# Packing a short inner tile, keeping four output pieces for the end, and pacing row loads in a three-stage decoder layer

## The chip, the cores and the metric

The kernel is one program on one core of a Trainium2 chip. Its engines are TensorE (PE in the profile; its weight loads are PEld), VectorE (DVE), ScalarE (ACT), GpSimd (POOL) and SyncE (SP), which here issues every DMA. The metric is the device time of one execution in microseconds; lower is better.

## The reference, cut to what matters

The input x is (8, 256, 1024), that is 2048 tokens of 1024 values. Three blocks follow each other, each added to the stream after a layer norm:

```python
x = x + attn(layernorm(x))        # 32 heads, 8 key/value heads; weights are sign(w), a scale per output channel
x = x + xattn(layernorm(x), ctx)  # low-rank cross attention, 16 heads
x = x + ffn(layernorm(x))

def bitnet_linear(x, weight, scale_param):
    s = jnp.maximum(jnp.mean(jnp.abs(weight), axis=1), 1e-08)
    return jnp.einsum('bsi,oi->bso', x, jnp.sign(weight / s[:, None])) * (s * scale_param)

def ffn(x):                       # U1 (1024, 256), V1 (256, 2*2752), U2 (2752, 256), V2 (256, 1024)
    H = (x @ U1) @ V1 + b1
    act = silu(H[..., :2752]) * H[..., 2752:]
    return (act @ U2) @ V2 + b2
```

The inner width 2752 is 21 tiles of 128 and one of 64.

## The kernel before, in words

The 2048 tokens are worked in four groups (`NG`) of 512 (`GT`). The three stages follow each other; the results of the first two pass through DRAM (`x1_scratch`, `x2_scratch`). One list, `ORDER`, sets the order of all work: `self_order`, `cross_order` and `ffn_order` write it by hand, and each engine's program walks through the same list and does its own share of every step, in that order, with semaphores between the engines. So a step that waits on an engine holds back all later steps of that engine, and that holds for SyncE's DMA issues too.

**Self-attention.** A group has 64 head steps (slots); work for the next group is put beside them by slot number (`put`). After each projection of queries or keys (`q_out`, `k_out`) its high and low float32r parts are copied by three DMAs of 256 KB into a stack (`q_stack`, `k_stack`) that the score matmuls (L804, L824) read. Row tiles of 512 KB (`load`, `wload`, `o_load`) go through two rings of buffers, `xin` and `x_res`. The channel scales of the v and o weights are needed as rows that are the same in all partitions: for each 128 channels VectorE makes a diagonal matrix (L1310) and TensorE multiplies ones by it (L755), four times for one PSUM bank; VectorE copies that out (L1332). For v (`row_v`) this happens in the start-up, for o (`row_o`) at the end of group 0, between the last queries (L790) and the keys of group 1 (L765). Two PSUM banks are then in turn for all such steps.

**Feed-forward.** A float32 product is done as three float32r matmuls (`PASSES`: high by high, high by low, low by high). For each group: `down` (48 matmuls), then for each of 22 inner tiles `gu` (gate and up, one bank each, 12 matmuls, L1002), SiLU on ScalarE (L1208), product on VectorE (L1513), high copy on ScalarE (L1212), low part on VectorE (L1516), and `z` (6 matmuls, L1014), which adds into two banks. TensorE does `gu` of a tile before `z` of the tile before it. The weights of each tile are split by ScalarE and GpSimd (`iw`: L1189, L1617) and by ScalarE and VectorE (`dw`: L1198, L1505). The short tile is padded with zeros, which GpSimd writes (L1596, L1614). At a group's end come `z` of the last tile and `z_out` (two copies L1220, two low parts L1522). The eight output pieces `y` of a group (6 matmuls each, L1027) stand in the first tiles of the next group; each `y_out` is two VectorE steps, row plus bias (L1533) and matmul plus row (L1536). Those of group 3 come at the end. `y_load` brings the rows (L1656), and a whole row of 512 KB is stored when its second piece is done (L1774, L1772).

Of the kernel before, what the change touches and what calls it, by code (L numbers as in the profile page):

```python
# [14 lines left out]
P = 128  # L15
# [31 lines left out]

AHEAD = 3
# [54 lines left out]
def self_order():  # L103
# [18 lines left out]
    order += signs(VB + 1) + flip_sign(VB) + with_inside(q_parts(0, 0), 4, flip_sign(VB + 1))  # L122
# [8 lines left out]
    for g in range(NG):  # L131
# [12 lines left out]
        if g == 0:  # L144
# [71 lines left out]
        if g == 0:  # L216
            order += [("row_o", 0), ("row_o_out", 0), ("row_o", 1), ("row_o_out", 1)]
# [80 lines left out]
def ffn_order():  # L298
    order = [("u2_zero",), ("iw_load", 0), ("b1_load",), ("iw_load", 1)]
# [6 lines left out]
    for g in range(NG):  # L306
        plan = {f: [] for f in range(FB)}
        if g:
            for i in range(2 * TILES):
                plan[i + 1].append([("y", g - 1, i), ("y_out", g - 1, i)])  # L310
                if i in (1, 3):
                    plan[i + 2].append([("y_load", g - 1, i // 2 + 2)])
# [13 lines left out]
        plan[FB - 2].append([("y_load", g, 0)])  # L326
        plan[FB - 1].append([("y_load", g, 1)])
        if g == NG - 1:
            plan[FB - 1] += [[("y_load", g, 2)], [("y_load", g, 3)]]
        for f in range(FB):  # L330
# [53 lines left out]
def row_buffers():  # L384

    out, before, last, count = {}, {}, {}, {"xin": 0, "xres": 0}
    for step in ORDER:
# [5 lines left out]
        elif step[0] in ("o_load", "v2_load") or step in (("u1_load", 0), ("raw_load", 1)):  # L393
            ring = "xres"
        elif step[0] == "y_load":
            ring = "xin" if step[1] == NG - 1 and step[2] >= 2 else "xres"
        else:
            continue
# [22 lines left out]
XSTACK = ordinals("xq_out")  # L421
STORES = {}
# [23 lines left out]
def build_program(nc, x, ctx_in, wq, qs, wk, ks, wv, vs, wo, os_, wq_d, w_qk, wkv_d, wv_u,  # L446
# [6 lines left out]
    def semaphore(name):  # L453
# [93 lines left out]


    names = ("consts scale_landed scale_mixed scale_cols abs chan mean_dve sign sign_set diag row_set "
# [5 lines left out]
             "u2_zero b1_zero b1_landed b1_set b2_landed u1_hi u1_lo p_hi p_lo v2_hi v2_lo "  # L555
             "iw_zero iw_hi iw_lo dw_hi dw_lo gate_up silu inner inner_hi inner_lo z_done z_hi z_lo y_dve").split()
# [19 lines left out]
    def copied_out(kind, *at):  # L576
# [31 lines left out]
        return sem["y_dve"], 2 * (at[0] * 2 * TILES + at[1]) + 2  # L608
# [97 lines left out]

    RAW_SPLIT = {1: 2, 0: 3, 2: 4, 3: 5}
    ROW_FIRST = {"v": (VB, KT), "o": (OB, KB)}
    row_numbers = {("v", 0): 0, ("o", 0): 1, ("o", 1): 2}
    diag_first = {("v", 0): 0, ("o", 0): KT, ("o", 1): KT + 4}  # L710


    def tensor_program(e):
        pe = e.eng
        for kind, *at in ORDER:
# [30 lines left out]
            elif kind in ("row_v", "row_o"):  # L746
                which = kind[-1]
                J, full, use = bank_of(kind + "_out", *at)
                n = min(4, ROW_FIRST[which][1])
                e.wait_ge(sem["consts"], 4)  # L750
                bank_free(e, kind + "_out", *at)
                for i in range(n):
                    d = diag_first[which, at[0]] + i
                    e.wait_ge(sem["diag"], d + 1)
                    t = pe.matmul(J[:, i * P:(i + 1) * P], ones[:, :], tmp[d % 2][:, 0:P], start=True, stop=True)  # L755
                    t.then_inc(full, 1) if i == n - 1 else t.then_inc(sem["row_set"], 1)
# [234 lines left out]
            elif kind == "gu":  # L991
# [4 lines left out]
                for s in range(2):  # L996
# [7 lines left out]
                    t.then_inc(sem["gate_up"], 1)  # L1004
            elif kind == "z":
# [6 lines left out]
                for r in range(RB):  # L1012
                    for wp, ap in PASSES:
# [4 lines left out]
            elif kind == "y":  # L1018
# [6 lines left out]
                for r in range(RB):  # L1025
                    for wp, ap in PASSES:
                        t = pe.matmul(J[:, :], zT[ap][:, r, m * P:(m + 1) * P], v2s[wp][:, r, n * GT:(n + 1) * GT],  # L1027
# [4 lines left out]
    def scalar_program(e):  # L1032
        act = e.eng
        for kind, *at in ORDER:
# [145 lines left out]
            elif kind == "iw":  # L1180
                g, f = at
                W = g * FB + f
                n = P if f < FB - 1 else FLAST
# [3 lines left out]
                if n < P:  # L1187
                    e.wait_ge(sem["iw_zero"], 2 * (g + 1))
                act.activation(v1s[W % 3][0][:, :, :, 0:n], inner_gu(f, n), ACT.Copy).then_inc(sem["iw_hi"], 1)  # L1189
            elif kind == "dw":  # L1190
                g, f = at
                W = g * FB + f
                e.wait_ge(iw_landed[f // CB], iw_total(f // CB))
                if W > 2:
                    e.wait_ge(sem["z_done"], W - 2)
                if f == FB - 1:
                    e.wait_ge(sem["u2_zero"], 1)
                act.activation(u2s[W % 3][0][:, :, :], u2_all[:, f, :].rearrange("p (r n) -> p r n", r=RB),  # L1198
                               ACT.Copy).then_inc(sem["dw_hi"], 1)
            elif kind == "gu":  # L1200
                g, f = at
                W = g * FB + f
                a = inner[W % 2]
# [4 lines left out]
                act.activation(a[:, :], bank[2 * W % 4][:, :], ACT.Silu, bias=b1c[:, f:f + 1]).then_inc(sem["silu"], 1)  # L1208
# [3 lines left out]
                act.activation(inner_hl[W % 2][:, 0, :], a[:, :], ACT.Copy).then_inc(sem["inner_hi"], 1)  # L1212
            elif kind == "z_out":
                g = at[0]
                e.wait_ge(sem["z_done"], FB * (g + 1))
                if g:
                    _, full, use = bank_of("y_out", g - 1, 2 * TILES - 1)
                    e.wait_ge(full, use + 1)
                for r in range(RB):
                    act.activation(zT[0][:, r, :], z_banks[r][:, :], ACT.Copy).then_inc(sem["z_hi"], 1)  # L1220

    def iw_total(c):
        return 16 * (3 if (c + 1) * CB * P <= INTER else 4)
# [16 lines left out]
    def vector_program(e):  # L1240
        dve = e.eng
        for kind, *at in ORDER:
# [54 lines left out]
            elif kind in ("row_v", "row_o"):  # L1297
                which = kind[-1]
                first, n = ROW_FIRST[which]
                for i in range(min(4, n)):  # L1300
                    idx = first + 4 * at[0] + i
                    d = diag_first[which, at[0]] + i
                    e.wait_ge(sem["chan"], SIGN["sign", idx] + 1)
                    e.wait_ge(sem["consts"], 3)
                    if which == "o" and i < 2:
                        _, full, use = bank_of("row_o_out" if at[0] else "row_v_out", 0)
# [520 lines left out]
```

## Time and profile before

| | |
|---|---|
| runs | 1490.9 us median of 3 (1489.54 to 1490.96) |
| the profiled execution's own time | 1487.3 us |
| its span, first to last instruction | 1485.5 us |
| TensorE busy | 1361.7 us (92%) |
| VectorE, ScalarE, GpSimd busy | 908.5, 709.9, 516.5 us |
| mean granted TensorE clock | 0.993 |

The profiled execution is one execution, recorded by the hardware; busy times are unions of the instructions of an engine. A matmul's recorded duration includes the passage through the array, so in a stream they overlap: 512-column matmuls of 0.39 us start closer together than that. A number in square brackets behind a timeline row is the idle time of the engine just before it and what ended it.

### The profile page before, as it was taken

To read this page: it belongs to the slowest core of one execution; us is meant where nothing else is said; L and a number is where in the kernel's file an instruction comes from. 1 tells how busy PE (TensorE), PEld (TensorE's weight loads), DVE (VectorE), ACT (ScalarE), POOL (GpSimd) and SP (SyncE) were. 2 spreads that over 40 slices of the span, in tenths; PEclk is the share of its full clock that TensorE was granted. 3 is DMA by queue.
4 is the path that set the end of the run, shared out by engine and by line. 5 is a ranking of instruction groups with operands and counts; after the bars stand their busy time and mean duration, and the time that the engine had idled before them with its cause. 6 is when DMAs were issued, how large, how long until landed. Compare 5 with 4: busy or idle time off the path is not lost.

```text
span 1485.5 us, 22620 instructions
## 1 busy us (share of the span) xinstructions
PE 1361.7 (92%) x8423; PEld 969.2 (65%) x8423; DVE 908.5 (61%) x1615; ACT 709.9 (48%) x1589; POOL 516.5 (35%) x457
## 2 busy tenths in 40 slices
PE   6788899899989998898889798778999999999998
PEld 4555455545555555557667676667888887887886
DVE  5578556835683668667486584663754754763645
ACT  4376503540354145437567475664544354354352
POOL 2047503760476156602121121123432432342230
PEclk9999899999999999999999999999999999999999
DMA  5786645665548455365546364436300310310121
GB/s 150 143 167 130 117 78 123 94 96 107 111 76 121 108 111 114 102 194 151 153 102 171 92 169 111 129 100 232 136 10 15 116 41 1 114 57 1 71 71 57
DMA packets 94881, 157.55 MB, mean 106 GB/s; under 512 B 9910, under 2 KB 49076, under 8 KB 94772
## 3 DMA queue, kind: packets, MB, share of 16 engines
q1 hardware_dynamic: 94772, 156.11, 44.1%
q8 instruction: 67, 1.10, 0.3%
q14 instruction: 42, 0.34, 0.1%
HBM read 82.15 MB, written 25.17 MB: 72 GB/s over the span
## 4 chain that ended last, share of the span: by engine, by line
PE 65%; DVE 12%; DMA 10%; ACT 5%; issue 5%; SPq 2%; POOL 1%; DVEq 0%; POOLq 0%; ACTq 0%
PE bank L1002 16%; PE bank L1014 8%; PE bank L918 7%; DMA q_stack<-hi_lo 5%; PE bank L790 5%; PE bank L903 3%; PE bank L744 3%; PE bank L824 3%; PE bank L839 2%; PE bank L804 2%; PE bank L1027 2%; PE bank L876 2%; PE bank L987 2%; PE bank L888 2%; PE bank L765 2%
## 5 line engine op out<-in xcount | busy, mean ns | idle before, releaser
L1556 POOL TENSOR_TENSOR fold<-wide 128x512 f32<-128x512 f32 x128 | 164.1, 1291 | 240.5 <-ACT wide L1082 221.3
L1082 ACT ACTIVATE wide<-bank 128x512 f32<-128x512 f32 x256 | 151.3, 597 | 141.7 <-PE bank L824 139.5
L1617 POOL TENSOR_TENSOR v_lo<-v_all,v_hi 128x512 fp32r<-128x512 f32 x88 | 122.7, 1395 | 233.6 <-ACT v_hi L1189 233.6
L1364 DVE TENSOR_REDUCE neg_top<-bank 128x2 f32<-128x512 f32 x256 | 171.0, 681 | 52.9 <-PE bank L804 51.5
L824 PE MATMUL bank<-q_stack,k_stack 98*128 98x512 f32 x256 | 138.4, 541 | 3.4 <-ACT wide L1082 2.6
L1002 PE MATMUL bank<-pT_hi,v_hi 128*128 128x512 f32 x352 | 137.3, 390 | 1.2 <-POOL v_lo L1617 1.2
L1002 PE MATMUL bank<-pT_hi,v_lo 128*128 128x512 f32 x352 | 137.2, 390 | 0.0
L1002 PE MATMUL bank<-pT_lo,v_hi 128*128 128x512 f32 x352 | 136.9, 389 | 0.0
L1513 DVE SCALAR_TENSOR_TENSOR inner<-bank,b_cols,inner 128x512 f32<-128x512 f32 x88 | 65.9, 749 | 111.3 <-PE bank L1002 108.0
L804 PE MATMUL bank<-k_stack,q_stack 96*128 96x256 f32 x512 | 111.0, 304 | 15.4 <-DMA q_stack<-hi_lo 9.7
L1099 ACT ACTIVATE wide<-bank,neg_max 128x256 f32<-128x256 f32 x256 | 120.0, 488 | 7.3 <-DVE neg_max L1392 7.3
L804 PEld LDWEIGHTS bank<-k_stack,q_stack 96*128 96x128 f32 x512 | 93.0, 193 | 44.1 <-DMA q_stack<-hi_lo 15.1
L1212 ACT ACTIVATE inner_hl<-inner 128x512 fp32r<-128x512 f32 x88 | 55.6, 632 | 135.3 <-DVE inner L1513 135.3
L1014 PE MATMUL bank<-inner_hl,u_hi 128*128 128x512 f32 x352 | 111.4, 397 | 3.7 <-DVE inner_hl L1516 3.7
L1593 POOL TENSOR_TENSOR x_group<-x_group,tmp 128x512 f32<-128x512 f32 x32 | 41.8, 1306 | 193.8 <-DVE tmp L1473 193.8
L1392 DVE TENSOR_REDUCE neg_max<-bank 128x2 f32<-128x512 f32 x128 | 86.8, 683 | 34.5 <-PE bank L876 33.8
L790 PE MATMUL bank<-hT_hi,signs_qkv 128*128 128x512 f16 x256 | 100.1, 391 | 5.0 <-DVE signs_qkv L1266 5.0
L1516 DVE TENSOR_TENSOR inner_hl<-inner,inner_hl 128x512 fp32r<-128x512 f32 x88 | 65.0, 739 | 61.5 <-ACT inner_hl L1212 61.5
L1208 ACT ACTIVATE inner<-bank,b_cols 128x512 f32<-128x512 f32 x88 | 60.5, 687 | 82.2 <-PE bank L1002 82.0
L1564 POOL TENSOR_TENSOR bn<-bn,neg_half 128x1 f32<-128x1 f32 x48 | 30.4, 632 | 197.5 <-DVE bn L1282 197.4
L918 PE MATMUL bank<-signs_o,attnT_hi 128*128 128x512 f16 x256 | 97.5, 381 | 0.8 <-DVE tmp L1413 0.6
L790 PE MATMUL bank<-hT_lo,signs_qkv 128*128 128x512 f16 x256 | 98.0, 383 | 0.0
(178 smaller groups left out, 3114.5 us busy)
## 6 DMA issues: line engine op xcount, KB each, us to landing
q_stack<-hi_lo SPq DMA_DIRECT2D x96, 256.0 KB, 6.4
xin<-x_scratch SPq DMA_DIRECT2D x32, 512.0 KB, 4.6
xq_stack<-xhi_lo SPq DMA_DIRECT2D x128, 128.0 KB, 2.4
x_res<-in_x SPq DMA_DIRECT2D x21, 512.0 KB, 5.0
x_scratch<-x_res SPq DMA_DIRECT2D x16, 512.0 KB, 2.9
xin<-in_ctx SPq DMA_DIRECT2D x16, 512.0 KB, 4.7
x_res<-x_scratch SPq DMA_DIRECT2D x16, 512.0 KB, 4.2
x_group<-x_scratch SPq DMA_DIRECT2D x32, 256.0 KB, 3.3
```

The costliest lines, as they stand in the source:

```text
L790: t = pe.matmul(J[:, :], sW[:, kb, tq * P:(tq + 1) * P], hT[p][:, kb, :], start=kb == 0 and p == 0, stop=kb == KB - 1 and p == 1)
L804: t = pe.matmul(tops[n % 2][:, a * SEQ:(a + 1) * SEQ], qst[U % Q_STACKS][0:SUB, r, b * SEQ + a * P:b * SEQ + (a + 1) * P], kst[0:SUB, tq, ...
L824: pe.matmul(tiles[m % 2][:, :], kst[0:SUB + 2, tq, b * SEQ + kt * P:b * SEQ + (kt + 1) * P], qst[U % Q_STACKS][0:SUB + 2, 2 * hp:2 * hp + ...
L918: t = pe.matmul(J[:, :], OT[p][:, tq, m * P:(m + 1) * P], sWo[:, tq, n * GT:(n + 1) * GT], start=tq == 0 and p == 0, stop=tq == KB - 1 and ...
L1002: t = pe.matmul(G[:, :], v1s[W % 3][wp][:, s, r, :], pT[g % 2][ap][:, r, :], start=r == 0 and (wp, ap) == (0, 0), stop=r == RB - 1 and wp ...
L1014: t = pe.matmul(z_banks[r][:, :], u2s[W % 3][wp][:, r, :], inner_hl[W % 2][:, ap, :], start=f == 0 and (wp, ap) == (0, 0), stop=f == FB - ...
L1082: act.activation(PT[m % PT_RING][:, :], tiles[m % 2][:, :], ACT.Exp).then_inc(sem["tile_exped"], 1)
L1099: t = act.activation(Pb[:, a * SEQ:(a + 1) * SEQ], S[:, a * SEQ:(a + 1) * SEQ], ACT.Exp, bias=mx[:, a:a + 1], accum_out=total)
L1364: dve.tensor_reduce(neg_top[U % 2][:, r, b, :], tops[n % 2][:, :].rearrange("p (a b) -> p a b", a=QT), AX.X, ALU.max, negate=True).then_in ...
L1392: dve.tensor_reduce(neg_max[n % 4][:, 0:QT], scores[n % 3][:, :].rearrange("p (a b) -> p a b", a=QT), AX.X, ALU.max, negate=True).then_inc ...
L1556: pool.tensor_tensor(fold[f % FOLD_RING][:, :], PT[2 * f % PT_RING][:, :], PT[(2 * f + 1) % PT_RING][:, :], ALU.add).then_inc(sem["folded" ...
L1617: pool.tensor_tensor(lo[:, :, :, 0:n], inner_gu(f, n), hi[:, :, :, 0:n].bitcast(F32), ALU.subtract).then_inc(sem["iw_lo"], 1)
```

## The change

Inner tile: the short tile is worked as the 21st of 22 (`TILE_AT`). Its 64 gate and 64 up columns share one stationary operand and one bank: 6 matmuls. SiLU works on the first 64 partitions; VectorE adds the bias to the up half (partitions 64 to 127) in a step of its own, then multiplies. The high part lies in partitions 0 to 63 and the low part in 64 to 127 of one operand, and U2's 64 rows are loaded twice, so `z` has two passes: 4 matmuls. The zero fills go.

Ends of groups: `z` of a group's last tile and `z_out` come after `gu` of the next group's first tile. The `y` pieces start one tile later. The last four of group 2 are kept for the end: two stand ahead of the last `z`, two around `z_out`, whose results in group 3 go to a part of `hT3`, since `zT` is still read. The row-plus-bias steps are steps of their own (`y_bias`); most of those of the last eight rows lie in tiles 10 to 19 of group 3, the last two just ahead of the third piece of group 3. The last row is stored in two halves of 256 KB.

Scale rows: one VectorE step builds the diagonals for a whole bank (a broadcast product), one matmul of up to 512 columns follows. For v the diagonal comes earlier; for o the three steps stand in slots 51 to 53 and 60 to 62 of group 0.

Row loads: before each row load of x for groups 1 to 3, each of the context rows of group 0 and each weight row of o but the first, SyncE waits until the newest query or key stack issued has landed.

```diff
+TILE_AT = [*range(FB - 2), FB - 1, FB - 2]
...
+            for i, at in ((0, 51), (1, 60)):
+                put(at, ("diag_o", i))
+                put(at + 1, ("row_o", i))
+                put(at + 2, ("row_o_out", i))
...
-        if g == 0:
-            order += [("row_o", 0), ("row_o_out", 0), ("row_o", 1), ("row_o_out", 1)]
...
-            for i in range(2 * TILES):
-                plan[i + 1].append([("y", g - 1, i), ("y_out", g - 1, i)])
+            for i in range(2 * TILES if g + 1 < NG else TILES):
+                plan[i + 2].append([("y", g - 1, i), ("y_bias", g - 1, i), ("y_out", g - 1, i)])
...
+            elif g:
+                order += [("z", g - 1, FB - 1), ("z_out", g - 1)]
...
-        order += [("z", g, FB - 1), ("z_out", g)]
+    last = NG - 1
+    order += [("y", last - 1, 4), ("y", last - 1, 5), ("z", last, FB - 1), ("y_out", last - 1, 4), ("y_out", last - 1, 5)]
+    order += [("y_load", last, 3), ("y", last - 1, 6), ("z_out", last), ("y", last - 1, 7)]
+    order += [("y_out", last - 1, 6), ("y_out", last - 1, 7)]
     for i in range(2 * TILES):
-        order += [("y", NG - 1, i), ("y_out", NG - 1, i)]
+        if i == 2:
+            order += [("y_bias", last, 6), ("y_bias", last, 7)]
+        order += [("y", last, i), ("y_out", last, i)]
...
+AFTER_STACK = ({("load", "x", g, m) for g in range(1, NG) for m in range(TILES)}
+               | {("load", "c", 0, m) for m in range(TILES)}
+               | {("wload", OB + i) for i in range(1, KB)})
...
+                pe.matmul(J[:, 0:n * P], ones[:, :], tmp[number % 2][:, 0:n * P], start=True, stop=True).then_inc(full, 1)
...
-                for s in range(2):
+                halves = 2 if TILE_AT[f] < FB - 1 else 1
+                for s in range(halves):
...
-                    for wp, ap in PASSES:
+                    for wp, ap in PASSES if TILE_AT[f] < FB - 1 else ((0, 0), (1, 0)):
...
+                if f == FB - 1:
+                    up = inner[(W + 1) % 2][0:FLAST, :]
+                    e.wait_ge(sem["inner_lo"], W)
+                    e.wait_ge(sem["silu"], W + 1)
+                    dve.tensor_scalar(up, bank[2 * W % 4][FLAST:P, :], b1c[FLAST:P, FB + f:FB + f + 1], None,
+                                      ALU.add).then_inc(sem["up_set"], 1)
+                    e.wait_ge(sem["up_set"], g + 1)
+                    dve.tensor_tensor(a[0:FLAST, :], up, a[0:FLAST, :], ALU.mult).then_inc(sem["inner"], 1)
+                    e.wait_ge(sem["inner_hi"], W + 1)
+                    dve.tensor_tensor(b[FLAST:P, 0, :], a[0:FLAST, :], as_f32(b[0:FLAST, 0, :]),
+                                      ALU.subtract).then_inc(sem["inner_lo"], 1)
+                    continue
...
+                if step in AFTER_STACK:
+                    e.wait_ge(stacked[stack % 2], 48 * (stack // 2 + 1))
```

## Rows read from the trace of the kernel before

**Rows 1.** The page: span, and the first engine's busy time.
```profile
span 1485.5 us, 22620 instructions
PE 1361.7 (92%) x8423; PEld 969.2 (65%) x8423; DVE 908.5 (61%) x1615; ACT 709.9 (48%) x1589; POOL 516.5 (35%) x457
```
**Rows 2.** Stretches: length, busy and count per engine, granted clock, DMA share, GB/s.
```profile
1134.00:1246.00 112.00, 112.00 (x510) 92.51 (x509) 66.76 (x113) 51.10 (x98) 40.05 (x32) 1.00 0.16 57
...
173.00:206.00 33.00, 28.20 (x178) 17.65 (x177) 14.34 (x25) 3.02 (x5) 7.40 (x7) 0.84 0.61 85
317.00:350.00 33.00, 32.42 (x240) 17.94 (x239) 12.28 (x20) 8.64 (x15) 15.37 (x14) 1.00 0.89 130
```
**Rows 3.** Timeline, last inner tile of group 3: start, duration, engine, line.
```profile
1461.48 0.39 PE L1002 MATMUL bank<-pT_hi,v_hi 128*128 128x512 f32 x1
...
1463.97 0.39 PE L1002 MATMUL bank<-pT_hi,v_lo 128*128 128x512 f32 x1
...
1464.40 0.75 DVE L1513 SCALAR_TENSOR_TENSOR inner<-bank,b_cols,inner 128x512 f32<-128x512 f32 x1 [1.60 <-PE bank L1002]
...
1465.85 0.69 DVE L1516 TENSOR_TENSOR inner_hl<-inner,inner_hl 128x512 fp32r<-128x512 f32 x1 [0.70 <-ACT inner_hl L1212]
```
**Rows 4.** TensorE's timeline at the end of group 0; waits of L1014, 1100 to 1485.
```profile
1129.96 0.39 PE L1014 MATMUL bank<-inner_hl,u_lo 128*128 128x512 f32 x1
1131.22 0.73 PE L1014 MATMUL bank<-inner_hl,u_hi 128*128 128x512 f32 x2 [0.87 <-DVE inner_hl L1516]
...
  DVE inner_hl L1516: 8.7, 8
```
**Rows 5.** Timeline of the end: last z, first y, last y, last add.
```profile
1467.85 0.40 PE L1014 MATMUL bank<-inner_hl,u_lo 128*128 128x512 f32 x1
...
1470.26 0.50 PE L1027 MATMUL bank<-v_hi,zT_hi 128*128 128x512 f32 x1 [2.01 <-DVE zT_lo L1522]
...
1481.05 0.39 PE L1027 MATMUL bank<-v_lo,zT_hi 128*128 128x512 f32 x1
...
1481.71 0.69 DVE L1536 TENSOR_TENSOR xin<-bank,xin 128x512 f32<-128x512 f32 x1
```
**Rows 6.** TensorE's timeline at the ends of groups 0 and 1 of self-attention.
```profile
172.90 0.38 PE L790 MATMUL bank<-hT_lo,signs_qkv 128*128 128x512 f16 x1
...
180.85 2.44 PE L755 MATMUL bank<-tmp,ones 128*128 128x128 f32 x8 [1.13 <-DVE tmp L1310]
...
183.08 0.63 PE L765 MATMUL bank<-hT_hi,signs_qkv 128*128 128x512 f16 x1
...
200.18 0.72 PE L804 MATMUL bank<-k_stack,q_stack 96*128 96x256 f32 x4
...
325.96 0.38 PE L790 MATMUL bank<-hT_lo,signs_qkv 128*128 128x512 f16 x1
...
343.03 0.71 PE L804 MATMUL bank<-k_stack,q_stack 96*128 96x256 f32 x4 [0.58 <-DMA k_stack<-hi_lo]
```
**Rows 7.** Waits; landings: stack at 260.4, at 283.9, load at 262.4; norm.
```profile
PE bank L804 <- DMA q_stack<-hi_lo: 9.7, 11, 1.5
...
DMA to landing us min/median/max: 4.3/5.8/7.1
...
DMA to landing us min/median/max: 4.3/5.8/6.9
...
DMA to landing us min/median/max: 7.6/7.6/7.6
...
275.42 1.28 DVE L1276 BATCH_NORM_STATS2 bn<-xin 128x6 f32<-128x512 f32 x2
```
**Rows 8.** VectorE groups by line and shape, 1100 to 1470: count, busy, mean ns.
```profile
L1505 DVE TENSOR_TENSOR u_lo<-u_all,u_hi 128x256 fp32r<-128x256 f32 x71 | 41.3, 582 | 0.0
```
**Rows 9.** Landings: row loads, 1380 to 1420 (L1656); stores of rows (L1774).
```profile
DMA to landing us min/median/max: 3.3/3.9/5.4
...
DMA to landing us min/median/max: 2.6/2.6/3.3
```

More of the change, by code:

```diff
@@ L325, in ffn_order @@
                 plan[3 + CB * i].append([("v2_load", i)])
[L326 to L329, printed above, removed]
+        if g + 1 < NG:
+            plan[FB - 2].append([("y_load", g, 0)])
+            plan[FB - 1].append([("y_load", g, 1)])
+        else:
+            for i in range(2):
+                for h in range(2):
+                    plan[10 + 2 * i + h].append([("y_bias", g - 1, 4 + 2 * i + h)])
+            for m in range(3):
+                plan[10 + m].append([("y_load", g, m)])
+                for h in range(2):
+                    plan[14 + 2 * m + h].append([("y_bias", g, 2 * m + h)])
         for f in range(FB):
@@ L395, in row_buffers @@
         elif step[0] == "y_load":
-            ring = "xin" if step[1] == NG - 1 and step[2] >= 2 else "xres"
+            ring = "xin" if step[1] == NG - 1 and step[2] < 3 else "xres"
         else:
@@ L546, in build_program, with z_home @@
     z_banks = bank[4:6]
-    names = ("consts scale_landed scale_mixed scale_cols abs chan mean_dve sign sign_set diag row_set "
+    def z_home(g):
+        return zT if g < NG - 1 else [a[:, 0:RB, :] for a in hT3]
+    names = ("consts scale_landed scale_mixed scale_cols abs chan mean_dve sign sign_set diag "
              "row_copied ln_stat ln_pow ln_done y_applied split_hi split_lo stack_hi stack_lo v_set "
@@ L749, in tensor_program @@
                 n = min(4, ROW_FIRST[which][1])
+                number = row_numbers[which, at[0]]
                 e.wait_ge(sem["consts"], 4)
                 bank_free(e, kind + "_out", *at)
[L752 to L756, printed above, removed]
+                e.wait_ge(sem["diag"], number + 1)
+                pe.matmul(J[:, 0:n * P], ones[:, :], tmp[number % 2][:, 0:n * P], start=True, stop=True).then_inc(full, 1)
             elif kind == "k":
@@ L1207, in scalar_program @@
                     e.wait_ge(sem["inner_lo"], W - 1)
-                act.activation(a[:, :], bank[2 * W % 4][:, :], ACT.Silu, bias=b1c[:, f:f + 1]).then_inc(sem["silu"], 1)
+                n = P if f < FB - 1 else FLAST
+                act.activation(a[0:n, :], bank[2 * W % 4][0:n, :], ACT.Silu, bias=b1c[0:n, f:f + 1]).then_inc(
+                    sem["silu"], 1)
                 e.wait_ge(sem["inner"], W + 1)
@@ L1622, in sync_program @@
         sp = e.eng
-        reload = []
+        reload, stack = [], None
         for kind, *at in ORDER:
@@ L1658, in sync_program @@
                 g, kt = at
-                s = STACK[(kind, *at)]
+                s = stack = STACK[(kind, *at)]
                 b = hl[s % 2]
@@ L1764, in sync_program @@
                     sem["b2_landed"], 16)
+            elif kind == "y_out" and at == [NG - 1, 2 * TILES - 2]:
+                buf, land, count = row_of("y_load", NG - 1, TILES - 1)
+                e.wait_ge(*copied_out(kind, *at))
+                sp.dma_start(rows(out, NG * TILES - 1)[:, 0:GT], buf[:, 0:GT]).then_inc(last_stored[TILES - 1], 16)
             elif kind == "y_out" and at[1] % 2:
```

119 lines of the change are left out of this document (63 added, 56 removed).

## The prediction

> **What bounds the kernel now.** I read the page first: the span is 1485.5 us and TensorE is busy for 1361.7 of it [rows 1]. The table by stretches then shows where the rest lies. In the feed-forward stage TensorE never rests inside a group: 112.00 of 112.00 us [rows 2]. What is taken off TensorE there is taken off the time, as long as the other engines keep up. In the self-attention stage the stretches 173 to 206 and 317 to 350 hold the same steps, the ends of groups 0 and 1; the first has 28.20 us of TensorE at a mean granted clock of 0.84, the second 32.42 us at 1.00 [rows 2]. So something at the end of group 0 alone stops TensorE. The timelines name it, and the stalls at the ends of feed-forward groups too.
>
> **Part 1, the packed inner tile.** Matmuls of 512 columns follow each other every (1463.97 - 1461.48) / 11 = 0.2264 us [rows 3]. A tile costs 12 of them for gate and up and 6 for z. The short tile (64 of 128 columns real) goes to 6 and 4: 8 fewer in each of 4 groups, 32 x 0.2264 = 7.2 us, all on the path. Its other engines pay more. The usual chain behind the last up matmul is product, high copy, low part: from 1463.97 + 0.39 to 1465.85 + 0.69, 2.18 us [rows 3]. The packed one has no up matmuls that hide its SiLU and one more VectorE step (up plus bias, then the product), two steps of about 0.7 us (as the 0.75 and 0.69 us steps there): 3.6 us. In groups 0 to 2 the step z of this tile comes after a half of `down` (12 matmuls), z of the tile before (6) and the next gate and up (12): 30 x 0.2264 = 6.8 us of cover. In group 3 there is no `down`: 18 x 0.2264 = 4.1 us; laying the steps after each other with the bias step and `dw` in VectorE's queue I find it done some 0.2 us early. The tile before it now has 12 matmuls of cover, 2.7 us, against 2.2 us plus the wait's own cost. I take 0 for these, and up to 1.5 us lost in group 3. The zero fills on GpSimd go; nothing on TensorE waited for them in a full group [rows 2]: 0.
>
> VectorE steps with two inputs in SBUF are dearer when GpSimd works: the 128x256 low part of `dw` takes 582 ns in the mean over groups, where GpSimd splits the next weights [rows 8]. The Trainium skill (SBUF — State Buffer, "SBUF: two separate sides") says that such a VectorE step and a GpSimd step that reads SBUF take a shared port one after the other; the new product has two SBUF inputs where the old one had one. By that rule a packed chain could grow by one GpSimd split; the cover of groups 0 to 2 takes that in, and in group 3 GpSimd has no split left at that point, so the sum stays the same.
>
> **Part 2, the ends of groups.** Before, z of tile 21 follows z of tile 20 at once and waits for its inner values: 1129.96 + 0.23 to 1131.22, 1.03 us [rows 4]; and the line of z has that wait four times, once for each end of a group (8 entries, as the weight load waits too) [rows 4]. Now gate and up of the next group's first tile (2.7 us) stand between: the chain of 2.2 us is hidden. The three ends of groups 0 to 2 give 3.1 us; I see no term that could take more than 0.5 us of it back. The two z_out copies and their low parts now fall beside gate and up of tile 1: TensorE returned 1470.26 - 1467.85 - 0.23 = 2.2 us after the last z where nothing else was left [rows 5], and here it has 2.7 us of work: 0 paid.
>
> **Part 3, the tail.** Before, TensorE waits 1.03 us ahead of the last z and 2.2 us after it [rows 4, 5], 3.2 us. Now two y pieces of group 2 (12 matmuls, 2.7 us) cover the first and two more the second. Each y of group 3 needs its bank back, and row 3 of group 3 is loaded only when the store of a row of group 2 is through: 0.7 us for the add, 2.6 us for the store, 3.9 us for the load (3.3 to 5.4) [rows 9], two bias steps at 0.7: 8.6 us, where TensorE brings the third y of group 3 after six pieces of 1.36 us = 8.2 us. VectorE is then 0.4 us late and the second bank absorbs part. I put 0.5 us back, with 0 to 2.5 as the range. The bias steps leave the last pieces: the last matmul starts at 1481.05, the last add only at 1481.71 [rows 5], 0.27 us behind the matmul's end, which goes. The last store is 256 KB, not 512: 2.6 us to land now; I take 0.3 us off and nothing as the lower bound. Together 3.2 - 0.5 + 0.3 + 0.3 = 3.3 us.
>
> **Part 4, the scale rows.** TensorE's last q matmul starts at 172.90, then come the eight little diagonals and broadcasts by turns (to 183.08), and the first score of group 1 starts at 200.18: 27.3 us. At the end of group 1 the same two points are 325.96 and 343.03: 17.1 us, with a wait of 0.58 us for the key stack in it [rows 6]. The difference, 10.2 us, also holds the half clock (0.84 in the mean, [rows 2]). The work itself returns elsewhere: two matmuls of 512 float32 columns. Eight instructions for 512 columns took 2.44 us at the lower clock [rows 6], so about 0.9 to 1.2 us at full clock, 2.1 us for both, put where TensorE has no gap; 0.5 us for a wait on the diagonal, which is one slot (some 1.5 us) ahead. Net 10.2 - 2.6 = 7.6 us. The range is 5 to 9. The v row: it lies ahead of the wait for the first query stack in the start-up, gain 0.
>
> **Part 5, paced row loads.** SyncE's queue now waits for the newest stack's landing before a row load. What could it win? A stack of three transfers lands at most 7.1 us after its issue with a load issued right behind it, and 6.9 us without one [rows 7]: 0.15 us. TensorE's waits for query stacks number 11, 9.7 us in all [rows 7]; if all got 0.15 us shorter, 1.6 us, but only some have a load behind them. What could it lose? The load lands at 7.6 us after its issue now, about 1.2 us behind the stack; held, it starts when the stack is in and takes a load's own 3.3 us [rows 9], so it lands 2.1 us later. The load issued at 262.42 (landed 270.0) is read by the layer norm at 275.42 [rows 7]: 5.4 us of slack, 3.3 left. The next step in SyncE's queue is the following unit's top rows, some 8 us behind the load, longer than the hold of up to 6.5 us. So I take 0.5 us gained, from 3 lost to 2 gained. [...]
>
> **Sum.** 7.2 + 3.1 + 3.3 + 7.6 + 0.5 = 21.7 us. The profiled execution took 1487.3 us and becomes 1465.6; it lies 3.6 us under the median of the runs, 1490.9, so the median becomes 1469.2.
>
> **Rivals.**
> Not all of part 4 is had (chance 0.15): the row steps stand in slots where VectorE and two banks are shared with the sign turns, each in-order wait costs 1 to 2 us and a stretch of lower clock stays. Part 4 gives 2 and not 7.6: 1475.
> The packed tile frees TensorE but VectorE and ScalarE become the bound around it (0.08): for it speaks the chain of 3.6 us, against it 6.8 us of cover. All 7.2 us come back: 1476.
> The stacks gain more from pacing than the single landing shows, or lower clock at other places vanishes with them (0.12): 6 us more, 1463.
> The holds in SyncE's queue reach TensorE (0.04): some 16 row loads are held. From 21.7 / 16 = 1.4 us passed on per hold it decides; a late row blocks VectorE at the norm, the running maxima behind it and then the scores. With 2 us each, 32 lost against 21.7: 1501. The slack of 5.4 us speaks against it.
> The change does nothing to the time (0.02): the stalls only move, since everything behind a group's end waits for stacks anyway: 1490. Against it, group 1's end already runs in 17.1 us with only 0.58 us of such a wait.
> The forecast has 0.59.
>
> **Numbers.** 1469.2 with a range of 1462 to 1477: the terms' bounds give (7.2 - 1.5) + 2.6 + 1.0 + 5 - 3 = 11.3 us to 7.2 + 3.1 + 3.8 + 9 + 2 = 25.1 us, 1466 to 1480; I go down to 1462 for the third rival and cut above at 1477, since all low bounds at once are unlikely and the first two rivals lie within it. A difference under 0.2% (3 us) can't be told from none. Faster 0.94, same 0.02, slower 0.04.
>
> **What would show it.** In the profile after: 32 fewer 512-column matmuls in the feed-forward stage and groups there about 2 us shorter; no TensorE wait for the inner low part ahead of the z step; the last z followed by y at once; the first score of group 1 some 17 us after the last q matmul and no low clock there; stack landings near 6.9 us; layer norm steps with no wait for a row. Wrong would be: TensorE waiting for a row, for the diagonal by over 1 us, or for the packed tile's low part; VectorE waiting for the last row of group 3 by over 2 us.

## The result and the profile after

The changed kernel takes 1468.3 us in the median (1466.0 to 1474.8, 4 runs) where the kernel before takes 1490.9 beside it (1489.5 to 1492.1): a ratio of 0.9858, 95% interval 0.9835 to 0.9881. It is faster by 22.6 us, 1.4%, and the interval leaves no room for an equal time; 21.7 were forecast. Two later comparisons of the same kernel gave 0.9858 (0.9833 to 0.9884) and 0.9851 (0.983 to 0.9873).

The two profiled executions differ by less: 1487.3 and 1468.8 us, and the spans by the same 18.5. The profiled execution of before lay 3.6 us under its median. So the traces can account for 18.5 us; the rest is which executions were profiled.

The page of after (span; busy time, share and instructions of each engine) answers to [rows 1]: 46 matmuls fewer, but only 7.2 us less of TensorE. Most of the gain is idle time that went.

```profile
span 1467.0 us, 22531 instructions
PE 1354.5 (92%) x8377; PEld 962.5 (66%) x8377; DVE 915.4 (62%) x1612; ACT 709.9 (48%) x1589; POOL 514.9 (35%) x448
```

**By stage.** I took the same instruction in both traces as a mark. The first `down` matmul of the feed-forward stage starts at 1012.92 before and at 1009.08 after: 3.8 us gained in all that lies ahead. From there to the end it is 472.6 us before and 457.9 after: 14.7 us.

**A turn of the feed-forward stage.** The table by stretches (columns as in [rows 2]) from the first `down` of one group to that of the next, of before:

```profile
1101.60:1218.40 116.80, 115.93 (x525) 95.43 (x524) 68.46 (x114) 52.82 (x100) 40.05 (x32) 1.00 0.15 55
```

and of after:

```profile
1097.92:1211.57 113.65, 113.65 (x517) 93.91 (x516) 68.37 (x115) 52.96 (x100) 39.67 (x30) 1.00 0.15 56
```

There are 8 matmuls fewer and no idle time: 3.15 us less a turn, of which 8 x 0.2264 = 1.81 us are the packed tile. Of the other 1.34 us, 1.15 lie at the end of the group: about 1.04 us ahead of its last `z` and 0.11 us in the first pair of matmuls behind the wait, which takes 0.73 us and not 0.62 [rows 4]. The remaining 0.15 us lie in the middle of the turn of before, at a `z` whose low part is only just done when TensorE comes to it (1185.98 + 0.69 = 1186.67). The timeline of before shows the low part, the four transposes ahead of the `z` (the last starts at 1186.58), and the `z`, 0.15 us behind that start where others in the turn stand 0.03 us behind theirs:

```profile
1185.98 0.69 DVE L1516 TENSOR_TENSOR inner_hl<-inner,inner_hl 128x512 fp32r<-128x512 f32 x1 [0.70 <-ACT inner_hl L1212]
...
1186.25 0.60 PE L744 MATMUL bank<-ident,xin 128*128 128x128 f32 x4
...
1186.73 0.73 PE L1014 MATMUL bank<-inner_hl,u_hi 128*128 128x512 f32 x2
```

Both profiles of before have this place in two turns, and no kernel with the new order has it, padded or packed. So it goes with the order; which step of it was not tested.

The last stretch, from the first `down` of group 3 to the end, holds two short tiles and one end of a group besides the tail: 150.4 us before, 141.8 after, 8.6 us less, so the tail has 8.6 - 3.62 - 1.15 = 3.8 us.

**The tail.** The timeline of after (columns as in [rows 3]) answers to [rows 3] and [rows 5]: the packed tile in group 3, the last z, the first y of group 3, the bias steps of the last row, the third y of group 3, the last matmul, the last add.

```profile
1440.57 0.69 ACT L1239 ACTIVATE inner<-bank,b_cols 64x512 f32<-64x512 f32 x1 [0.99 <-PE bank L1032]
...
1441.39 0.76 DVE L1557 TENSOR_SCALAR inner<-bank,b_cols 64x512 f32<-64x512 f32 x1 [0.46 <-ACT inner L1239]
...
1443.57 0.69 DVE L1562 TENSOR_TENSOR inner_hl<-inner,inner_hl 64x512 fp32r<-64x512 f32 x1 [0.70 <-ACT inner_hl L1244]
...
1449.23 0.39 PE L1045 MATMUL bank<-inner_hl,u_lo 128*128 128x512 f32 x1
1449.46 0.39 PE L1058 MATMUL bank<-v_hi,zT_hi 128*128 128x512 f32 x1
...
1452.32 0.47 PE L1058 MATMUL bank<-v_hi,hT_hi 128*128 128x512 f32 x1
...
1456.00 1.28 DVE L1584 TENSOR_TENSOR x_res<-x_res,b_all 128x512 f32<-128x512 f32 x2
...
1457.94 0.50 PE L1058 MATMUL bank<-v_hi,hT_hi 128*128 128x512 f32 x1
...
1463.29 0.39 PE L1058 MATMUL bank<-v_lo,hT_hi 128*128 128x512 f32 x1
...
1463.79 0.69 DVE L1592 TENSOR_TENSOR x_res<-bank,x_res 128x512 f32<-128x512 f32 x1 [0.67 <-PE bank L1058]
```

The packed chain runs from 1440.57 to 1443.57 + 0.69 = 1444.26, 3.7 us, and its z starts at 1444.46 as soon as TensorE comes to it. The last z is followed by y without a gap. Where `hT3` is read first (1452.32), and where the bank of the row with the late bias steps comes back (1457.94), TensorE is 0.1 us late and its next matmul 0.1 us later still, 0.2 us lost each time.

**The scale rows.** The timeline of after around them: the two diagonals on VectorE, the first broadcast matmul, the last q matmul of group 0 and the first score of group 1. It answers to [rows 6].

```profile
161.54 1.66 DVE L1345 TENSOR_TENSOR tmp<-ident,channel_scale 128x512 f32<-128x512 f32 x1
...
163.35 1.10 PE L785 MATMUL bank<-tmp,ones 128*128 128x512 f32 x2 [1.79 <-DVE tmp L1345]
...
174.47 0.68 DVE L1345 TENSOR_TENSOR tmp<-ident,channel_scale 128x512 f32<-128x512 f32 x1
...
179.44 0.38 PE L819 MATMUL bank<-hT_lo,signs_qkv 128*128 128x512 f16 x1
...
196.73 0.71 PE L833 MATMUL bank<-k_stack,q_stack 96*128 96x256 f32 x4 [0.81 <-DMA k_stack<-hi_lo]
```

From the last q matmul to the first score it is 17.3 us where it was 27.3, and the granted clock of the stretch 173 to 206 is 1.00 where it was 0.84. But the last q matmul itself now comes at 179.44, not 172.90, 6.5 us later. Following matching matmuls, 2.5 us of this delay arise between 141 and 148 us, in a stretch of lower clock that this execution of before did not have, and 4.1 us at the two broadcasts; 2.6 us were forecast for these. Part 4 thus won 10.0 - 4.1 = 5.9 us.

### The profile page after: what moved, and what is told of

The parts are those of the page before. It is cut to its first block, busy times and chain, and to the rows that moved or that the text cites. A ratio compares the mean times of both kernels' runs of the same rounds, so it can differ in the third digit from the quotient of the medians.

```text
span 1467.0 us, 22531 instructions
## 1 busy us (share of the span) xinstructions
PE 1354.5 (92%) x8377; PEld 962.5 (66%) x8377; DVE 915.4 (62%) x1612; ACT 709.9 (48%) x1589; POOL 514.9 (35%) x448
## 4 chain that ended last, share of the span: by engine, by line
PE 67%; DVE 11%; DMA 9%; issue 5%; ACT 5%; SPq 2%; POOL 1%; DVEq 0%; POOLq 0%; ACTq 0%
PE bank L1032 15%; PE bank L1045 8%; PE bank L947 7%; DMA q_stack<-hi_lo 5%; PE bank L819 5%; PE bank L1058 3%; PE bank L932 3%; PE bank L775 3%; PE bank L868 3%; PE bank L853 3%; PE bank L833 2%; PE bank L905 2%; PE bank L1016 2%; PE bank L794 2%; PE bank L883 2%
## 5 line engine op out<-in xcount | busy, mean ns | idle before, releaser
L1665 POOL TENSOR_TENSOR v_lo<-v_all,v_hi 128x512 fp32r<-128x512 f32 (+1 forms) x88 | 124.0, 1410 | 232.4 <-ACT v_hi L1219 232.4
L1032 PE MATMUL bank<-pT_hi,v_hi 128*128 128x512 f32 x344 | 134.2, 390 | 1.5 <-POOL v_lo L1665 1.5
L1032 PE MATMUL bank<-pT_hi,v_lo 128*128 128x512 f32 x344 | 134.1, 390 | 0.0
L1032 PE MATMUL bank<-pT_lo,v_hi 128*128 128x512 f32 x344 | 133.8, 389 | 0.0
L833 PE MATMUL bank<-k_stack,q_stack 96*128 96x256 f32 x512 | 111.6, 305 | 14.8 <-DMA q_stack<-hi_lo 9.2
L1244 ACT ACTIVATE inner_hl<-inner 128x512 fp32r<-128x512 f32 (+1 forms) x88 | 55.6, 632 | 133.3 <-DVE inner L1566 126.8
L1566 DVE SCALAR_TENSOR_TENSOR inner<-bank,b_cols,inner 128x512 f32<-128x512 f32 x84 | 62.9, 749 | 86.3 <-PE bank L1032 85.6
L1239 ACT ACTIVATE inner<-bank,b_cols 128x512 f32<-128x512 f32 (+1 forms) x88 | 60.5, 688 | 79.4 <-PE bank L1032 79.3
```

The source lines that it names most:

```text
L833: t = pe.matmul(tops[n % 2][:, a * SEQ:(a + 1) * SEQ], qst[U % Q_STACKS][0:SUB, r, b * SEQ + a * P:b * SEQ + (a + 1) * P], kst[0:SUB, tq, ...
L1032: t = pe.matmul(G[:, :], v1s[W % 3][wp][:, s, r, :], pT[g % 2][ap][:, r, :], start=r == 0 and (wp, ap) == (0, 0), stop=r == RB - 1 and wp ...
L1665: pool.tensor_tensor(inner_home(W, 1), inner_gu(f, n), as_f32(inner_home(W, 0)), ALU.subtract).then_inc(sem["iw_lo"], 1)
```

## The experiments

All edits but one are made to the changed kernel, with one part undone or moved. Kernels of one comparison ran on one chip, beside the kernel before: 1488.7 us in the median in the first (17 runs), 1489.1 in the second (11 runs), 1490.6 in the third (8 runs). Intervals of ratios are about 0.0025 either way, some 4 us, so for terms of 1 to 4 us the traces decide and the times only must not contradict them.

**The changed kernel again** (no edit).

> The changed kernel once more, as the yardstick for the runs beside it and for a second profile. My theory: 0.985 of the kernel before, about 1468 us. In its first profile the low-clock stretches lay at other places than before the change (one of 6.8 us at 140.8, three of 3.4 us at 417, 434 and 568). If these belong to the change they come again at the same places within 1 us; if they depend on how an execution falls against the clock's own timing, some move or vanish and the self-attention stage changes by 1.5 to 3 us with each.

1468.4 us, ratio 0.9858 (0.9833 to 0.9884); the span of the profiled execution is 1470.4, its feed-forward stage 457.7 us from the first `down`, the 457.9 of the first profile within 0.2. The 3.4 us by which this span is longer lie in the stages ahead; the last part of this section comes back to them.

**No pacing.**

```diff
-AFTER_STACK = ({("load", "x", g, m) for g in range(1, NG) for m in range(TILES)}
-               | {("load", "c", 0, m) for m in range(TILES)}
-               | {("wload", OB + i) for i in range(1, KB)})
+AFTER_STACK = set()
```

> The changed kernel with the waits for the stacks ahead of row loads taken out, nothing else. My theory (transfers follow each other in the queue, so the pacing has nothing to win): within 1.5 us of the changed kernel, third transfer of a stack landing at 7.1 instead of 6.9 us. Rival (pacing speeds the stacks up and pays): 3 to 6 us slower than the changed kernel. Rival (the holds cost): 2 us or more faster.

1469.2 us, ratio 0.9861 (0.9832 to 0.9891), against 0.9858 with pacing.

**Pacing alone**: the kernel before with the set `AFTER_STACK` and its wait in SyncE's queue, nothing else.

> The kernel before with only the waits for the stacks ahead of row loads put in. My theory: no difference from the kernel before (within 0.1%, 1.5 us). Rival (pacing pays): 3 us or more faster. Rival (holds reach TensorE): slower.

1490.0 us over 12 runs, ratio 1.0003 (0.9983 to 1.0022). Both ways pacing is worth nothing that can be told. The waits by line say how little it touches, first of the kernel after, then of the kernel without pacing (us in total, times, longest):

```profile
PE bank L833 <- DMA q_stack<-hi_lo: 9.2, 11, 1.8
```

```profile
PE bank L831 <- DMA q_stack<-hi_lo: 9.9, 11, 1.6
```

And the median landings of the transfers issued from 255 to 300 us, of after and then without pacing (KB, us to landing):

```profile
q_stack<-hi_lo SPq DMA_DIRECT2D x9, 256.0 KB, 5.8
...
x_res<-in_x SPq DMA_DIRECT2D x1, 512.0 KB, 3.1
```

```profile
q_stack<-hi_lo SPq DMA_DIRECT2D x9, 256.0 KB, 5.8
...
x_res<-in_x SPq DMA_DIRECT2D x1, 512.0 KB, 7.6
```

A load behind a stack takes 7.6 us from its issue, a held one 3.1; the stacks take 5.8 us either way. So here the load that waits behind a stack does not slow the stack.

**The o rows at the end of group 0 again**, in the new form, one diagonal step and one broadcast for four blocks of 128 channels.

```diff
-            for i, at in ((0, 51), (1, 60)):
-                put(at, ("diag_o", i))
-                put(at + 1, ("row_o", i))
-                put(at + 2, ("row_o_out", i))
...
+        if g == 0:
+            order += [("diag_o", 0), ("row_o", 0), ("row_o_out", 0), ("diag_o", 1), ("row_o", 1), ("row_o_out", 1)]
```

> The changed kernel with the three steps of the o scale rows (in their new form: one diagonal step and one matmul per bank) put back to the end of group 0. TensorE then waits there for VectorE twice, about 0.7 + 0.1 + 1.1 + 0.1 + 0.75 us each, twice, perhaps at the lower clock, 5 to 7 us in all; and the 4 us that the steps cost in their slots (1.8 us of it the wait for the diagonal) come back. My theory: 1 to 4 us slower than the changed kernel, that is, a good part of the 10 us at the end of group 0 came from doing four diagonals and matmuls by turns, not from the place. Rival (the place is all): 8 us slower.

1474.2 us, ratio 0.9901 (0.9871 to 0.9931): 5.8 us slower than the changed kernel beside it. By the times that lies between what I expected of the theory and of its rival; the interval allows both. The timeline shows the last q matmul, both broadcasts and the first score of group 1:

```profile
174.91 0.38 PE L817 MATMUL bank<-hT_lo,signs_qkv 128*128 128x512 f16 x1
178.17 1.94 PE L783 MATMUL bank<-tmp,ones 128*128 128x512 f32 x2 [2.88 <-DVE tmp L1343]
181.79 2.05 PE L783 MATMUL bank<-tmp,ones 128*128 128x512 f32 x2 [1.67 <-DVE tmp L1343]
200.39 0.72 PE L831 MATMUL bank<-k_stack,q_stack 96*128 96x256 f32 x4
```

From the first to the last it is 25.5 us, with two waits for the diagonal, 4.6 us, and a low clock: the pair of 512-column matmuls takes 1.94 us and not 1.10. So of the 10 us the place made 25.5 - 17.3 = 8.2, with the low clock that comes there, and the new form alone gives 27.3 - 25.5 = 1.8. In their slots the steps cost 4.1 us, so moving them wins 8.2 - 4.1 = 4.1 us by the traces, at the upper end of the theory.

**The short tile padded again**, at its new place: 12 and 6 matmuls, the zero fills on GpSimd, one load of U2's rows, the usual chain of four steps.

```diff
...
-                halves = 2 if TILE_AT[f] < FB - 1 else 1
+                halves = 2
...
-                    for wp, ap in PASSES if TILE_AT[f] < FB - 1 else ((0, 0), (1, 0)):
+                    for wp, ap in PASSES:
...
+                    for a in v1s[W % 3]:
+                        pool.memset(a[:, :, :, :].bitcast(F32), 0.0).then_inc(sem["iw_zero"], 1)
...
```

> The changed kernel with the short inner tile padded with zeros again (12 and 6 matmuls, the zero fills and waits of before), all the rest of the change kept. My theory: 32 more matmuls of 0.2264 us on TensorE's path, 7.2 us slower than the changed kernel, the feed-forward stage longer by the same 7.2 us. Rival (the packed tile is bound by its chain on VectorE and ScalarE): under 4 us slower.

1477.4 us, ratio 0.992 (0.9891 to 0.9948): 9.2 us more than the changed kernel by the ratios, where 7.2 were expected and the intervals allow them. The same turn as above, in its table by stretches:

```profile
1104.66:1220.12 115.46, 115.46 (x525) 95.41 (x524) 67.67 (x114) 53.07 (x100) 40.42 (x32) 1.00 0.15 55
```

525 matmuls again and not a wait: 1.81 us more a turn than after, exactly 8 x 0.2264. Both kernels keep TensorE full here, so the packed tile costs no wait anywhere, and against before (116.80) this kernel shows what the new order is worth in a turn by itself: 1.34 us.

**The packed tile last** (order of tiles as before).

```diff
-TILE_AT = [*range(FB - 2), FB - 1, FB - 2]
+TILE_AT = [*range(FB)]
```

> The changed kernel with the packed tile as the last of 22, not next to last. Its chain of SiLU, bias step, product, high copy and low part measured 1440.57 to 1444.26, 3.7 us, in the changed kernel; behind it stands only gate and up of the next group's first tile, 2.7 us. My theory: TensorE waits about 1.0 us for it at the ends of groups 0 to 2 and in the tail, 3 to 4 us slower in all. Rival (place does not matter, since another engine's queue hides it): same within 1 us.

1471.1 us, ratio 0.9879 (0.9854 to 0.9904). Turns of 114.2 us, 0.55 more than after, and 142.8 instead of 141.8 us for the last part, 2.1 us in all, where 3 to 4 were expected. The wait is not the expected one either. The timeline shows the end of the packed chain, its `z`, and the `z` of the next group's first tile:

```profile
1127.91 0.69 DVE L1562 TENSOR_TENSOR inner_hl<-inner,inner_hl 64x512 fp32r<-64x512 f32 x1 [0.70 <-ACT inner_hl L1244]
...
1128.79 0.39 PE L1045 MATMUL bank<-inner_hl,u_hi 128*128 128x512 f32 x1
...
1131.44 1.28 DVE L1575 TENSOR_TENSOR zT_lo<-bank,zT_hi 128x512 fp32r<-128x512 f32 x2
...
1132.87 0.70 PE L1045 MATMUL bank<-inner_hl,u_hi 128*128 128x512 f32 x2 [0.28 <-DVE zT_lo L1575]
```

The packed chain is done at 1128.60 and its `z` starts at 1128.79 without a wait. Late is the next `z`, which needs the banks that `z_out` empties (1131.44 + 1.28 = 1132.72). So theory and rival both fail: the place of the packed tile matters, but by 2 us, not by its 7, and in the turns through `z_out`.

**z of the last tile at once**, ahead of the next group's first tile, as before.

```diff
-            elif g:
-                order += [("z", g - 1, FB - 1), ("z_out", g - 1)]
...
+        if g + 1 < NG:
+            order += [("z", g, FB - 1), ("z_out", g)]
```

> The changed kernel with z of a group's last tile and z_out ahead of the next group's first tile again (the tail as changed). The last tile's z then has only the z of the packed tile, 4 matmuls (0.9 us), to cover its chain. My theory: a wait of about 1.5 us at each of three ends, 4.5 us slower. Rival (the first gate and up was held by something else, and the stall only moves): within 1 us of the changed kernel.

1474.2 us, ratio 0.9903 (0.988 to 0.9925). Its turns are 115.3 us and its last part 143.4, each 1.6 more than after, 4.8 us in all; its waits from 1100 us on:

```profile
PE bank L1045 <- DVE inner_hl L1569: 4.0, 3, 1.3
```

Three waits of 1.3 us: the wait of [rows 4] with its name, so the stall does not merely move and the rival falls. The timeline has the other 0.3 us:

```profile
1122.43 0.39 PE L1045 MATMUL bank<-inner_hl,u_lo 128*128 128x512 f32 x1
1124.15 0.73 PE L1045 MATMUL bank<-inner_hl,u_hi 128*128 128x512 f32 x2 [1.33 <-DVE inner_hl L1569]
```

From start to start 1124.15 - 1122.43 - 0.23 = 1.49 us are lost, more than the idle time of 1.33, which counts only from the end of the overlapping matmul; the first pair behind the wait adds 0.11. Together they are the 1.6.

**No piece of group 2 kept for the end**: all eight inside group 3.

```diff
-            for i in range(2 * TILES if g + 1 < NG else TILES):
+            for i in range(2 * TILES):
...
```

> The changed kernel with all eight y pieces of group 2 inside group 3 (tiles 2 to 9), so that nothing covers the last z and z_out. My theory: TensorE waits 1.5 us ahead of the last z (0.9 us of cover instead of 1.36) and 2.2 us behind it, against 0.4 us in the changed kernel: 3.3 us slower. Rival (the tail is bound by the last rows' loads and VectorE adds anyway): under 1 us slower.

1473.0 us, ratio 0.9894 (0.9871 to 0.9918). Its last part takes 145.6 us and not 141.8, 3.8 more, where 3.3 were expected; the rival falls. Both waits of before are back in the waits of the last part:

```profile
PE bank L1053 <- DVE hT_lo L1570: 2.0, 1, 2.0
PE bank L1040 <- DVE inner_hl L1564: 1.4, 1, 1.4
```

**The first diagonal of o earlier**: slot 46 instead of 51.

```diff
-                put(at, ("diag_o", i))
+                put(at - 5 if i == 0 else at, ("diag_o", i))
```

> Kernel after, with the first diagonal of o in slot 46 of group 0 instead of 51; its matmul stays in slot 52. In the profile after, this diagonal took 1.66 us on VectorE and TensorE waited 1.79 us for it at 163.35; the second one took 0.68 us and cost 0.12 us. Theory (the moved steps cost 4.1 us instead of the forecast 2.6 because the diagonal comes too late): the wait at the first row matmul falls from 1.8 us to under 0.3 us and the kernel is about 1.5 us faster than the kernel after. Rival (TensorE is ahead of the query stacks and key stacks anyway there): the wait goes, another one behind it grows by as much, 0 us. Both lie within what the run-to-run spread of the time can hide, so the waits in the trace decide: the wait of the row matmul, and the time from the first row matmul's slot to the last q matmul of the group.

1466.6 us, ratio 0.9831 (0.9809 to 0.9852), beside 1469.1 and 0.9851 (0.983 to 0.9873) for the changed kernel. The timeline, first diagonal and first broadcast:

```profile
155.12 0.68 DVE L1345 TENSOR_TENSOR tmp<-ident,channel_scale 128x512 f32<-128x512 f32 x1
...
162.92 1.13 PE L785 MATMUL bank<-tmp,ones 128*128 128x512 f32 x2
```

The wait of 1.79 us is gone and nothing takes its place: ahead of it matmuls start 1.2 us later than in the profile of after, and from it to the first score of group 1 they start 0.3 to 0.4 us earlier. The rival, another wait behind it, falls. The diagonal itself took 0.68 us instead of 1.66. The gain in time, 2.4 us, agrees with 1.8, but the intervals overlap; by the trace this is the best version here.

**Both kernels once more, for a second profile of before and a third of after.**

> The kernel after once more, beside e6 on the same chip, and a third profile of it. Theory (short stretches of lower clock at recurring places fall in some executions and not in others): 1468 us again within 2 us, with low-clock stretches at some of the places 45, 141, 161, 291, 418 to 421, 434 to 438, 568 to 571, 745, 833, 932, 980, 1025, in another selection than in the two profiles before. Rival (the selection belongs to the kernel): the same selection as in one of them.

> The kernel before once more, a second profile of it. Theory: the 10 us at the end of group 0 of self-attention are a matter of the order of steps, so the two points (last q matmul, first score of group 1) lie 25 to 28 us apart again against 17 in the kernel after, whether or not a low-clock stretch falls there. Rival: the low clock there made most of it; without it they lie 20 us apart or less.

After: 1469.1 us as above. The first diagonal took 1.66 us again and TensorE waited 1.78 us. Before: 1489.1 us, and the end of group 0 reads as in [rows 6], 201.85 - 174.51 = 27.3 us, as the theory has it:

```profile
174.51 0.38 PE L790 MATMUL bank<-hT_lo,signs_qkv 128*128 128x512 f16 x1
...
201.85 0.72 PE L804 MATMUL bank<-k_stack,q_stack 96*128 96x256 f32 x4
```

The granted clock from 176.5 to 184.9 was 0.51 there and 0.50 in the first profile. The lower clock at this place goes with the waits: of 13 profiles the four whose broadcasts stand there have it, and none of the other nine. So its share is not separated from theirs. Two numbers bound it: it lasts 10.2 us in both profiles of before and at half clock costs at most half of that, which leaves 22 us and not the rival's 20; and in the kernel with pacing alone, where it lasts 6.8 us, the two points still lie 200.62 - 174.09 = 26.5 us apart.

The clock elsewhere does not belong to the kernel. The stretch from 140 to 148 us in the three profiles of the changed kernel, and that from 417 to 421 in the first and the third (the granted clock is the third number from the right):

```profile
140.00:148.00 8.00, 6.38 (x37) 3.66 (x37) 4.62 (x10) 4.02 (x8) 4.30 (x4) 0.58 0.49 172
417.00:421.00 4.00, 3.90 (x22) 2.15 (x26) 1.66 (x4) 1.55 (x3) 3.22 (x4) 0.59 0.39 135
```

```profile
140.00:148.00 8.00, 6.20 (x55) 4.13 (x56) 6.32 (x14) 5.86 (x12) 5.06 (x6) 1.00 0.52 179
```

```profile
140.00:148.00 8.00, 7.00 (x40) 4.06 (x41) 4.02 (x9) 4.37 (x7) 4.45 (x5) 0.57 0.25 87
417.00:421.00 4.00, 3.51 (x36) 1.89 (x34) 3.42 (x8) 2.11 (x5) 3.91 (x4) 1.00 0.41 133
```

The same program falls to 1.2 GHz there in one execution and not in the next, and the third profile has another selection of such places than either of the two before. The theory on them holds, its rival does not. The stretch of 6.8 us at 141 cost 2.5 us. One of 3.4 us at 1024, in the third profile alone, cost 1.5: from the first `down` of group 0 to that of group 1 it is 90.4 us there and 88.9 in the first profile.

## Why the prediction was right, step by step

**Part 1, 7.2 us forecast.** Right: 1.81 us in each turn, and 145.4 against 141.8 us in the last part, which holds two short tiles, 7.2 us in all. The padded version shows that nothing is paid back: without and with packing TensorE has no wait in a turn. The packed chain was forecast at 3.6 us and took 3.7, and was done 0.2 us before TensorE came to its `z` in group 3, as forecast; the loss of up to 1.5 us in group 3 did not come, and the rival of VectorE as the bound has fallen.

**Part 2, 3.1 us forecast, 3 x 1.15 = 3.5 measured.** The mechanism was right and the term a little too small: I priced the wait of one end at 1.03 us, and left out that the first pair of matmuls behind a wait takes longer (0.73 against 0.62 us). Another 2 x 0.15 = 0.3 us came from the place in mid-turn, which no term of mine had. The padded version, which has the old tile and the new order, measures both together, 1.34 us a turn.

**Part 3, 3.3 us forecast, 3.8 measured.** The experiment without kept pieces gives 3.8 too, but by another sum, so the agreement is luck: it keeps the smaller last store, and its first wait is 0.5 us longer than that of before, since only the 4 matmuls of the packed tile cover it. From start to start the two waits of before cost 3.4 us with their first pairs, where I had 3.2. I put 0.5 us back for late rows, and 0.4 remained: 0.2 at the row with the late bias steps, which stand in VectorE's queue without a wait for their load (1456.00), and 0.2 at the first read of `hT3`, for which I had nothing. The last add starts 0.50 us behind the start of the last matmul where it was 0.66, so 0.16 and not 0.27; the smaller last store lands in 2.0 us instead of 2.6, so 0.6 and not 0.3. 3.4 - 0.4 + 0.2 + 0.6 = 3.8 us.

**Part 4, 7.6 us forecast, 5.9 measured.** The 10 us at the end of group 0 were right (10.0). The term that was mis-sized is the work that returns: 4.1 us, not 2.6. The two matmul pairs are 2.2 us as forecast at 2.1; the wait for the diagonal was put at 0.5 and is 1.79 + 0.12. So one of my own signs of being wrong came, a wait for the diagonal by over 1 us. Two things make it. I took the diagonal to be one slot ahead, some 1.5 us, but in VectorE's order it stands behind a copy (L1301, 160.93 to 161.62) that itself waits 0.79 us for TensorE. So it begins at 161.54, when TensorE has already come to the broadcast (163.35 - 1.79 = 161.56): with 0.68 us, the length of the second one, the wait would still be some 0.8 us. The rest, 1.0 us, is its length of 1.66 us. The experiment with the earlier diagonal takes the wait away, late start and length together.

For the length, GpSimd's timeline of after shows the two steps beside each of the two diagonals:

```profile
160.16 2.49 POOL L1611 TENSOR_TENSOR fold<-wide 128x512 f32<-128x512 f32 x2
...
173.24 3.03 POOL L1611 TENSOR_TENSOR fold<-wide 128x512 f32<-128x512 f32 x2
```

At 161.54 the second GpSimd step is already 0.15 us under way; it takes its usual 1.27 us, and the diagonal ends 0.55 us behind it. At 174.47 both start within 0.01 us: the diagonal takes 0.68 us and GpSimd's step 1.81 instead of 1.27. All three profiles of the changed kernel show both cases. At 155.12, in the version with the earlier diagonal, no GpSimd step runs (one ends at 154.40, the next begins at 155.88), and neither is lengthened. That one of the two engines waits for the other, and not always the same one, is what the Trainium skill (SBUF — State Buffer, "SBUF: two separate sides") says of a VectorE step with two SBUF inputs and a GpSimd step that reads SBUF. I had weighed that rule only for the packed tile, where it did not act (the new product took 683 ns in the mean of its four), and not for the diagonal, which is also a step with two SBUF inputs. I did not vary GpSimd alone, so the cause of the length is argued from these rows; that the wait costs 1.8 us is shown.

**Part 5, 0.5 us forecast.** Nothing by two experiments (0.9858 against 0.9861, and 1.0003). The held load is in 11.5 us after the stack's first issue (264.90 - 256.59 + 3.2) where it was 9.6 (262.42 - 260.44 + 7.6), 1.9 us later where I had 2.1. No cost of the holds shows in the times, so the rival with 1501 us has fallen, and the one with more gained from pacing too. The rival with 1501 us was also counted wrongly: `AFTER_STACK` holds 12 + 4 + 7 = 23 loads, not some 16, so it would have decided from 0.9 us a hold.

**The sum.** Measured in the traces: 7.2 + 3.5 + 0.3 + 3.8 + 5.9 + 0 = 20.7 us; the spans differ by 18.5. The feed-forward part closes: 14.8 of terms against 14.7. Ahead of it 5.9 us should be seen and 3.8 are. Followed by matching matmuls, the changed kernel is 3.5 us ahead at 200 us (5.9 less the 2.5 of the lower clock at 141), 6.7 at 410, 3.1 at 440 and 3.8 at the mark. Of the 3.2 gained up to 410, 1.6 fall on the lower clock that before has at 298 us; the 3.6 lost up to 440 fall on the two stretches that after has at 417 and 434. The other 1.6 up to 410 and the 0.7 gained behind 440, in spite of the stretch at 567, have no term in the forecast, and no run separates them: that part stays open.

The forecast of 1469.2 for the median was met at 1468.3 with errors of opposite sign: part 4 1.7 too much, pacing 0.5 too much, parts 2 and 3 1.2 too little. That it came within 1 us is in part luck. The rest lies within what the medians of before differ by from one comparison to the next (1488.7 to 1490.9). The rival "not all of part 4 is had" was right in kind (a wait on the diagonal that is too late) but not in size.

## What to carry to other kernels

Where a step moves into a running schedule, look when its producer's engine comes free at the new place and which engines work beside it. Here a VectorE step with two SBUF inputs had to stand several slots ahead of its reader, five where it was tried, since it began late and ran beside GpSimd. A wait on the path cost its idle time plus some 0.3 us here (0.87 by its row and 1.15 in all, 1.33 and 1.60), so filling the ends of groups is worth a little more than the waits add up to. When a part is moved and costs less than expected, look which wait it made: putting the packed tile last cost 2 us, and the wait was at another step. Before DMA issues are paced, compare the landing of the transfer ahead with and without one behind it: where it does not move, there is nothing to win.

## What I had not expected of the hardware

The granted clock: at recurring places (near 141, 161, 291, 419, 436 and 570 us in this kernel) it is at half in some executions and not in others of the same program, for 3.4 to 6.8 us, which alone moves a span by a few microseconds. Near 45 us it is at half in all 13 profiles. One profile of each kernel can't place a difference of 3 us in these stages.

The same VectorE instruction of 128x512 float32 took 1.66 us at 161.54 and 0.68 at 174.47 in one execution, and 0.68 at 155.12 in the version that has it earlier. At 174.47 GpSimd's step beside it was the longer one, 1.81 us against 1.27.

A 512 KB load issued behind a stack took 7.6 us and a held one 3.1, and the stack ahead 5.8 us in both cases.
